# Scores of a quaternion attention over one head's 32 partitions, and the third batch's expert tiles beside the last batch's dense experts

## The reference, cut to what matters

```python
def _L1_attn_ref(x, ...):                       # quaternion attention
    q = quat_norm(quat_linear(x, qW, qb))
    k = quat_norm(quat_linear(x, kW, kb))
    v = quat_linear(x, vW, vb)
    # 16 heads of 8 features
    scores = jnp.einsum('bthd,bshd->bhts', q_, k_) * scale
    scores = scores + jnp.mean(jnp.sin(J[:T])) * 0.1
    attn = jax.nn.softmax(scores, axis=-1)
    out = jnp.einsum('bhts,bshd->bthd', attn, v_).reshape(B, T, D)
    return quat_linear(out, oW, ob)

def _L1_ffn_ref(x, gate_w, w1, b1, w2, b2):     # 8 experts, each token takes 2
    probs = jax.nn.softmax(jnp.einsum('bsd,ed->bse', x, gate_w), axis=-1)
    topk_probs, topk_idx = jax.lax.top_k(probs, 2)
    h = jax.nn.gelu(w1 of the expert @ x + b1)  # 128 -> 512
    y = w2 of the expert @ h + b2               # 512 -> 128
    return jnp.sum(y * topk_probs[..., None], axis=-2)
```

## Time and profile before

| | |
|---|---|
| median of 3 runs | 1028.57 us (1026.48 to 1032.39) |
| the profiled execution, its own time | 1028.42 us |
| its span, first to last instruction | 1026.6 us |
| granted TensorE clock, mean | 0.914 |
| PE, DVE, ACT, POOL busy | 788.0, 558.1, 486.0, 288.4 us |

### The profile page before, as it was taken

One profiled execution on the slowest core, in us unless ns is written; L12 is line 12 of the kernel. 1 busy time (PEld: TensorE's weight loads), 2 busy tenths in 40 slices (PEclk: granted clock), 3 DMA queues, 4 the chain that ended last, 5 costly groups with the idle time before them and its releaser, 6 DMA issues.

```text
span 1026.6 us, 21722 instructions
## 1 busy us (share of the span) xinstructions
PE 788.0 (77%) x8393; PEld 567.9 (55%) x8393; DVE 558.1 (54%) x1728; ACT 486.0 (47%) x1035; POOL 288.4 (28%) x366
## 2 busy tenths in 40 slices
PE   1688886778887889888989786976667576765896
PEld 0577765656665566665566552754426453365575
DVE  3255566466655374545374724776645366298145
ACT  1234352325544547754557525778343365434332
POOL 3200101000333020233020234553273675046400
PEclk9989999799998999997999988999876788889899
DMA  4400200001100001000001011010110110101100
GB/s 122 135 2 2 117 2 3 1 1 28 38 2 11 2 12 42 2 23 12 9 5 32 12 40 44 27 34 12 49 52 23 47 47 8 34 28 36 40 11 21
DMA packets 32530, 29.89 MB, mean 29 GB/s; under 512 B 9230, under 2 KB 26404, under 8 KB 32300
## 3 DMA queue, kind: packets, MB, share of 16 engines
q1 hardware_dynamic: 30636, 25.23, 8.6%
q0 software_dynamic: 1536, 3.15, 1.1%
q10 hardware_dynamic: 256, 0.13, 0.0%
HBM read 11.44 MB, written 8.52 MB: 19 GB/s over the span
## 4 chain that ended last, share of the span: by engine, by line
PE 49%; DVE 26%; issue 9%; ACT 8%; POOL 3%; ACTq 1%; another core or an unknown queue 1%; POOLq 0%; SPq 0%; DMA 0%; DVEq 0%
PE ps L1522 5%; PE ps L1667 5%; PE ps L1537 4%; PE ps L1682 4%; PE ps L1525 4%; PE ps L1450 3%; PE ps L1550 3%; PE ps L1767 3%; PE ps L1758 3%; DVE probsT L973 3%; PE ps L1617 2%; PE ps L1519 2%; ACT late L901 2%; DVE neg_max L1160 2%; DVE stats L1006 2%
## 5 line engine op out<-in xcount | busy, mean ns | idle before, releaser
L901 ACT ACTIVATE late<-ps,j_bias 128x512 f32<-128x512 f32 x256 | 173.6, 693 | 193.6 <-PE ps L1667 170.7
L1160 DVE TENSOR_REDUCE neg_max<-ps 128x2 f32<-128x32 f32 (+31 forms) x128 | 90.4, 706 | 148.2 <-PE ps L1528 144.1
L611 POOL TENSOR_SCALAR q_heads<-q_heads,head_mask 128x512 fp32r<-128x512 f32 x64 | 100.6, 1588 | 206.0 <-DMA q_heads<-q_half 205.9
L1667 PE MATMUL ps<-q_heads,k_parts 128*128 128x512 f32 x256 | 138.7, 558 | 17.1 <-ACT late L901 14.1
L828 ACT ACTIVATE probs<-ps,neg_max 128x16 f32<-128x16 f32 (+31 forms) x256 | 108.9, 483 | 26.5 <-DVE neg_max L1160 26.2
L752 ACT ACTIVATE probsT<-ps 128x128 f32<-128x128 f32 (+3 forms) x128 | 55.8, 436 | 127.3 <-PE ps L1537 113.7
L1522 PE MATMUL ps<-kT_two,q_wide 64*64 64x262 f32 (+16 forms) x1024 | 74.2, 354 | 36.3 <-DVE probsT L973 24.7
L973 DVE COPY probsT<-ps 128x128 f32<-128x128 f32 (+3 forms) x173 | 74.8, 432 | 48.2 <-PE ps L1537 24.8
L1537 PE MATMUL ps<-ident,probs 128*128 128x128 f32 x640 | 97.5, 284 | 1.0 <-ACT probs L828 1.0
L635 POOL TENSOR_TENSOR q_wide<-qT,eighth_mask 128x1024 f32<-128x1024 f32 x16 | 31.2, 1948 | 228.8 <-PE ps L1528 167.6
L1667 PEld LDWEIGHTS ps<-q_heads,k_parts 128*128 128x128 f32 x256 | 50.8, 206 | 66.6 <-ACT late L901 45.2
(11 more groups left out here) (259 smaller groups left out, 1424.4 us busy)
## 6 DMA issues: line engine op xcount, KB each, us to landing
k_parts<-k_half SPq DMA_DIRECT2D x64, 64.0 KB, 2.0
q_heads<-q_half SPq DMA_DIRECT2D x64, 64.0 KB, 2.0
x_by_expert<-q_heads SPq DMA_DIRECT2D x3, 960.0 KB, 7.6
probsT<-x_by_expert SPq DMA_DIRECT2D x45, 64.0 KB, 1.8
y_by_expert<-probsT SPq DMA_DIRECT2D x45, 64.0 KB
late<-in_L_ffn_w_dram SPq DMA_DIRECT2D x1, 2048.0 KB
w_in<-in_L_ffn_w_dram SPq DMA_DIRECT2D x1, 2048.0 KB
x_all<-in_L_attn_x_dram SPq DMA_DIRECT2D x4, 256.0 KB, 5.3
```

The costliest lines, as they stand in the source:

```text
L611: last = pool.tensor_scalar(q_heads[:, hg % 2, g, :], together.bitcast(f32), head_mask[:, g:g + 1], None, ALU.mult)
L901: nc.scalar.activation(head_probs[:, i % SLOTS, :], ps[:, banks[i % len(banks)], :], ACT.Exp, bias=j_bias[:]).then_inc(e2_ready.sem, 1)
L1160: nc.vector.tensor_reduce(neg_max[:, n % 4, :], ps[:, k:k + OCT, 0:QS * (n + 1)], axis=AXX, op=ALU.max, negate=True).then_inc(max_ready.se ...
L1667: mm(ps[:, banks[i % R], :], k_parts[:, hg, kc * P:(kc + 1) * P], q_heads[:, hg % 2, g, :], start=True, stop=True).then_inc(s2_ready.sem, 1)
```

## The change

1. `spread_group` writes the four combinations onto every fourth partition (`parts[c:P:4]`), for k and for q (`q_parts`, new, one place per group). A head's 8 features x 4 combinations then lie on 32 neighbouring partitions, and the score product takes those 32 alone. The masks on POOL, `heads_apart` and `q_heads` go. Groups 0 to 2 are spread at slot 52, group 3 at the last slot.
2. X of batch 1 runs in round 5 from slot 6 on in every third slot.
3. Behind round 5, N of batch 3 comes first; two pieces of X of batch 2 stand beside its last two pieces, and three stand behind each piece of D. This batch (`BY_GELU`) uses ACT's gelu directly: one ACT pass from PSUM in place of L933, L1336, L1338, L925, L1319.
4. D's up products rotate over two banks (0, 5), the down products over 6 and 7. The gelu table is loaded at the end of N of batch 3. C moves: batch 1 behind D pieces 0 to 2, batch 2 behind 5 to 7.

```diff
@@ plan
-                put(r, 12, "X", 1, NX, 2)
+                put(r, 6, "X", 1, NX, 3)
@@
-        for k in range(max(NX, RANKED)):
-            if k < RANKED:
-                yield ("N", LAST)
-            if k < NX:
+        for k in range(RANKED):
+            yield ("N", LAST)
+            if k >= RANKED - 2:
                 yield ("X", LAST - 1)
         for k in range(NE):
             yield ("D", LAST)
-            if k in (0, 2, 3):
+            yield from [("X", LAST - 1)] * 3
+            if k in (0, 1, 2):
                 yield ("C", LAST - 2)
-            if k in (1, 4, 5):
+            if k in (5, 6, 7):
                 yield ("C", LAST - 1)
@@ sync
+            def spread_group(b, hg):
+                if b:
+                    sp.wait_ge(s2_ready.sem, s2_ready.at(b - 1, (hg + 1) * GH * KC))
+                for c in range(4):
+                    for half, parts, which, done in ((k_half, k_parts, c // 2, k_spread), (q_half, q_parts, c % 2, q_spread)):
+                        sp.dma_start(parts[c:P:4, hg, :].bitcast(f32),
+                                     half[hg * GR:(hg + 1) * GR, which, :].bitcast(f32)).then_inc(done[hg].sem, 16)
@@ gpsimd
-            def heads(b, hg):
...
-                for g in (1, 2, 3, 0):
-                    last = pool.tensor_scalar(q_heads[:, hg % 2, g, :], together.bitcast(f32),
-                                              head_mask[:, g:g + 1], None, ALU.mult)
-                last.then_inc(heads_apart.sem, 1)
@@ scalar, by_expert
-                    if 0 <= n < NT:
+                    if 0 <= n < NT and b != BY_GELU:
...
-                                                        ps[:, 1 + (b * NT + n) % 2, m * P:(m + 1) * P], ACT.Identity,
+                                                        ps[:, 1 + (b * NT + n) % 2, m * P:(m + 1) * P],
+                                                        ACT.Gelu_apprx_tanh if b == BY_GELU else ACT.Identity,
@@ tensor, quat
-                            pe.wait_ge(heads_apart.sem, heads_apart.at(b, hg + 1))
+                            pe.wait_ge(q_spread[hg].sem, q_spread[hg].at(b + 1, 0))
...
-                        mm(ps[:, banks[i % R], :], k_parts[:, hg, kc * P:(kc + 1) * P], q_heads[:, hg % 2, g, :],
+                        rows = slice(g * GR, (g + 1) * GR)
+                        mm(ps[:, banks[i % R], :], k_parts[rows, hg, kc * P:(kc + 1) * P], q_parts[rows, hg, :],
```

More of the change, by code:

```diff
@@ L495, in spread @@
                 sp.wait_ge(k_half_ready.sem, k_half_ready.at(b, 1))
+                sp.wait_ge(q_half_ready.sem, q_half_ready.at(b, 1))
                 for hg in range(HG - 1):
-                    spread_k(b, hg)
-                sp.wait_ge(q_half_ready.sem, q_half_ready.at(b, 1))
-                spread_q(b, 0)
+                    spread_group(b, hg)
                 yield
[L501 to L511, removed]
+                spread_group(b, HG - 1)
                 yield
@@ L553, in all_experts @@
                 yield
-            take({"S": spread, "Q": quat, "X": by_expert, "C": sums, "D": all_experts})
+            take({"S": spread, "X": by_expert, "C": sums, "D": all_experts})
             sp.wait_ge(x_stored.sem, x_stored.at(B, 0))
@@ L717, in sums @@
                 yield
-            take({"R": relative, "A": attention, "W": weights, "S": spread, "Q": quat, "N": norm, "X": by_expert,
-                  "C": sums})
+            take({"R": relative, "A": attention, "W": weights, "N": norm, "X": by_expert, "C": sums})
         def copy_pT(eng, copy, o, done, b, n):
@@ L950, in all_experts @@
                             act.wait_ge(moe_y_ps.sem, e - 1)
-                        nc.scalar.activation(moe_h[:, e % 2, m, :], ps[:, n % NUP, :], ACT.Gelu_apprx_tanh,
+                        nc.scalar.activation(moe_h[:, e % 2, m, :], ps[:, UP_BANKS[n % NUP], :], ACT.Gelu_apprx_tanh,
                                              bias=b1T[:, m, e:e + 1]).then_inc(moe_h_ready.sem, 1)
+                    if e == 0:
+                        act.wait_ge(gatesT_ps.sem, 1)
+                        copy(gates_T, ps[0:NE, DOWN_BANKS[1], :].rearrange("p (t s) -> p t s", t=T)
+                             ).then_inc(gatesT_ready.sem, 1)
                     yield
@@ L1329, in by_expert @@
                             dve.wait_ge(y_stored[(b * NT + n) % 2], 16 * ((b * NT + n) // 2))
-                        nc.vector.scalar_tensor_tensor(out=yx[:, (b * NT + n) % 2, :], in0=wc[:, (b * NT + n) % 4, W3:W3 + P], scalar=2.0,
+                        nc.vector.scalar_tensor_tensor(out=yx[:, (b * NT + n) % 2, :], in0=wc[:, (b * NT + n) % 4, W3:W3 + P],
+                                                       scalar=1.0 if b == BY_GELU else 2.0,
                                                        in1=ps[:, AM, 0:P], op0=ALU.mult, op1=ALU.add
@@ L1742, in by_expert @@
                     if 0 <= n < NT:
-                        pe.wait_ge(hx_ready.sem, hx_ready.at(b, n + 1))
+                        if b == BY_GELU:
+                            pe.wait_ge(hb_ready.sem, hb_ready.at(b, n + 1))
+                        else:
+                            pe.wait_ge(hx_ready.sem, hx_ready.at(b, n + 1))
                         if b * NT + n:
@@ L1772, in all_experts @@
                 pe.wait_ge(e2_ready.sem, e2_ready.at(B, 0))
-                pe.wait_ge(hb_ready.sem, hb_ready.at(LAST, 0))
+                pe.wait_ge(attn2_ready.sem, attn2_ready.at(B, 0))
                 up(0)
+                pe.wait_ge(b7_free, fill_no["N", LAST, 9] + 1)
                 pe.wait_ge(gates_ready.sem, 1)
                 for t in range(T):
-                    last = nc.tensor.transpose(ps[0:NE, 3, t * P:(t + 1) * P], gates[:, t, :], ident[:])
+                    last = nc.tensor.transpose(ps[0:NE, DOWN_BANKS[1], t * P:(t + 1) * P], gates[:, t, :], ident[:])
                 last.then_inc(gatesT_ps.sem, 1)
@@ L1780, in all_experts @@
                 for t in range(T):
-                    last = mm(ps[:, 3, t * P:(t + 1) * P], gates_T[:, t, :], b2_sb[:], start=True, stop=True)
+                    last = mm(ps[:, DOWN_BANKS[1], t * P:(t + 1) * P], gates_T[:, t, :], b2_sb[:], start=True, stop=True)
                 last.then_inc(accb_ps.sem, 1)
                 for e in range(NE):
+                    yield
                     if e + 1 < NE:
```

67 lines of the change are left out of this document (18 added, 49 removed).

## The result

The kernel after takes 1057.78 us (median of 4 runs, 1054.02 to 1059.97), the kernel before 1030.05 beside it: a ratio of 1.0269 with a 95% interval from 1.0223 to 1.0314. It is 28 us slower, where 13 us faster was forecast, and lies outside the range. A second set of runs gave 1.0299 (1.0237 to 1.0361).

The account below looks back on a forecast made before the run. PE was taken to bound rounds 2 and 3, waits round 5. From 1028.4 us, +17 (score shape) - 2 (masks) - 20 (round 5) - 8 (tail) = -13 gave 1015 us, range 990 to 1036.

Parts of the forecast that it names:

- the sum's first term: Scores on PE: shape changes cost 0 to 34 us; half, +17, taken because the chain is on PE 49% of the span.
- The shape's price for one score: On PE, a 32-row score between two 128x128 products costs about 0.29 us more; next product 0.40 or more behind.
- rival (b): Rounds 2 to 4: shape changes lie fully on the path, the kernel gets slower, about 1045 us; chance 0.15.
- a cold clock in round 5 on 10 of them: Slower rival's addition to 34 us of shape changes: round 5's low clock (0.79) repeats; together taken as 40 us.
- The growth by over 10 us and the clock under 0.88: Signs of a wrong forecast: rounds 2 to 4 each grow over 10 us, or their granted clock falls below 0.88.
- parts 2 and 3: Round 5 (wider tile spacing, mask wait gone), 20 us less, and the new order behind it, 8 us less.
- Nothing is saved on PE: Scores on PE: the same 256 products of 512 columns remain, so no PE time is gained.
- The masks: POOL's mask work beside DVE's small steps lengthens some of them; its going saves 2 us (0 to 5).
- Off the chain nearly everywhere: POOL's mask work, 16 groups of 6.2 us, 99 us in all, hardly stands in the chain.
- Round 5: Fewer waits for tile weights, earlier weight copies and wider tile spacing: 20 us less (8 to 28).
- The tail: Behind round 5: the last norm begins at 1010 against 1018.9, 8 us less.
- 2.2 more: Behind round 5: batch 1's gathers, standing before tile 5, add 2.2 us to the groups of X pieces.

Follow-up runs that it names:

- row means: Ratios to the kernel before, averaged over four plans (old, wider spacing, new tail, both): masked 128-row scores 0.995, zeroed tiles 0.985, 32-row scores 1.026.
- zeroed tiles: Kernel before, masks replaced by DMAs putting each head's queries on its own 32 partitions of otherwise zero tiles, full 128-row products: 0.9818; with new plans 0.9827 to 0.9885.
- old plan: Round 5 spacing and tail left as in the kernel before; with only the scores changed, 32 rows gave 1.0297, DMA-filled zero tiles 0.9818.
- The 64 rows: Kernel after with score products over 64 rows, each summing two heads' scores (output not the reference's): 1045.85 us, ratio 1.0236.
- the pair of added products: Kernel after with one more product ahead of each score in rounds 4 and 5: on 128 rows 1059.79 us (1.0367), on 32 rows 1075.37 us (1.0458).
- without the plans: Kernel before with the 32-row scores alone, its round 5 and tail as they were: 1056.58 us, ratio 1.0297.
- the spacing: Kernel before, masks kept, with only the new wider spacing of the tiles in round 5: 1022.79 us, ratio 0.9941.
- the plans alone: Kernel before with the wider tile spacing in round 5 and the new tail, masked 128-row scores kept: 1019.91 us, ratio 0.9915.
- the new tail alone: Kernel before, masks kept, with only the new order of work behind round 5: 1024.95 us, ratio 0.9941.

## Why the prediction was wrong

**The step that failed** is the sum's first term, "I take half, 17 us", and that the clock was left out of it. On the path the 32-row score costs about 4.1 of 100 (row means 1.026 to 0.985), 42 us; the single pairs of ratios give 28 to 49. Cut by rounds, scores on 32 rows against zeroed tiles, old plan: 6.4, 8.9, 24.2, 9.1, then 3.7 behind the last score.

- The shape's price for one score was right: 0.28 us between 128*128 neighbours, forecast 0.29, with the next product 0.43 behind the score and the score 0.20 behind the last product (forecast 0.40 or more, and 0.20). PE's busy time grows by 10.8 and 13.4 us in rounds 2 and 3, more than the forecast's 34 us over four rounds would give. But "half, because PE holds half the chain" used an average over the span. Rounds 2 and 3 are bound by PE, and 15.3 of these 24 us lay on the path; in round 3 the clock had a share in it (0.93 against 0.97).
- The clock was a repeat in rival (b), at 0.15 with shape changes, as "a cold clock in round 5 on 10 of them". It fell in round 4 already (0.88 to 0.74). The growth by over 10 us and the clock under 0.88, which the prediction named as signs of being wrong, both show in that round, and in no other of the three. Two thirds of the loss are in rounds 4 and 5, where the old clock already went up and down. The 64 rows, and the pair of added products, show that the fall goes with the rows of the score. The earlier trace rows showed that the clock was already low there (0.79 in round 5); the step from "a quarter of the array's rows" to "less of what keeps the clock" was missing.
- (b) named the right side and the first cause; its place, rounds 2 to 4, holds three quarters of the loss. Its sum is added up wrongly: 1028 + 40 - 2 - 14 is 1052, not 1045. That its 40 is near the 42 is in part luck, as it took 34 for the shape and 6 for the clock in round 5, while the larger part of the loss is where the clock fell. The gains of parts 2 and 3, taken there at half, come to nothing measurable on 32-row scores (1.0297 without the plans, 1.0269 and 1.0299 with them).
- "Nothing is saved on PE" was not quite so: the 26 pairs of scores in rounds 4 and 5 that ran at once saved PE 0.3 us or more each, since two 128-row scores start 0.31 to 0.34 us apart at the upper clock; that makes 8 us of PE as an estimate. It was lost beside the rest.

**The masks** were priced at 2 us, beside what of them was in round 5. Their going is worth about 1 in 100 of the time (row means 0.995 to 0.985), 10 us; single pairs give 6 to 19. Between before and the zeroed tiles 10.8 of these were in round 5, 5.5 in round 4. "Off the chain nearly everywhere" was read from where POOL stands in the chain; what a mask did to the steps behind it does not stand there. Which steps these were is not shown: the xn wait of 8.2, now 4.6, is 4.8 with the masks in and the tiles spaced wider.

**Round 5**, forecast -20 with its mask's going: -5 (1022.79 against 1027.67) from the spacing, and nothing once the masks are gone. The named wait for POOL did go, but PE then waits 12.4 for the same products by another name. The two gains don't add (1004.99 us without the masks, 1015.81 with the wider spacing too); that both edits take away the same slack is the likely reason, not a shown one. In the kernel after this wait is 4.7, under the 9 forecast, and the round is still longer (142.2 against 136.4).

**The tail**, forecast -8: from the first transposes of N to the end of the span the plans alone take 130.5 us in place of 137.6, which is -7.1, and the new tail alone gave -3 (1024.95 against 1027.67). The kernel after takes 133.0 and shows the steps. Its chain:

```profile
943.60 1.73 PE ps L1695 x8
945.33 4.93 PE ps L1718 x8
...
958.21 11.11 another core or an unknown queue
...
976.62 3.62 PE ps L1718 x8
980.25 3.57 PE ps L1729 x32
983.93 0.89 PE ps L1695 x8
...
990.46 3.62 PE ps L1718 x8
```

N's first transposes are at 923.76, so the first tile is 20 behind them (forecast 19.5); a piece of D takes 7.19 (7.2), a group of three tiles 6.5 (6.4). The step that was off is batch 1's gathers ahead of a tile's weights, "2.2 more": DVE stands still for 11.1, ACT for 7.9 and PE for 4.0. On POOL:

```profile
958.76 0.97 POOL L666 DMA_INDIRECT q_rel<-y_by_expert,row_no  x1
...
968.49 0.61 POOL L650 COPY probsT<-w1T 128x512 f32 x1
```

Eight gathers, 9.7 us, stand between the weights of two tiles, and it is only behind them that DVE goes on; the profile doesn't name what it waits for. The last norm starts 125.3 behind N (forecast 121, before 129.9); DVE ends its weighted sums 5.8 us after PE's last product (forecast 6).

**What stays open.** Kernels whose work is the same up to a point came out 4 to 10 us apart in single rounds of their profiles. Mostly the longer round had the lower clock, but not in round 4 of the zeroed tiles (149.4 us at 0.85, 145.1 at 0.84); what decides it was not found. How the 33 us of rounds 4 and 5 split between shape and clock was not measured either. So the sizes of the spacing's and the tail's gains (0 to 6 us), and which plan is best on zeroed tiles, are not settled. Settled is the sign of the rest: 32-row scores cost 28 us or more against zeroed tiles with the same plan, and all four kernels with zeroed tiles are faster than both the kernel before and the one after (ratios 0.982 to 0.989).

## What to carry to other kernels

Before a matmul is cut to fewer rows, look at what it saves and at what it takes away. Alone it saved nothing here (0.50 us on 32 rows, 0.48 on 128); it saves only where the next one on another strip stands right behind it, which a plan must arrange. What it takes away is the continuity of shape with its neighbours, paid on both sides, and the part of PE's work that holds the granted clock, paid by every product around it. Look for the second cost in the stretches where the clock already moves, not in the full ones. If data must be kept apart by head, let the DMA that moves it anyway write into zeroed tiles, and keep the full-row product. And an engine that is off the chain is not free: price it by the waits behind it, and don't add two gains that may close the same wait.

## What the runs showed of the hardware

- A score between 128*128 products costs 0.28 us more on 32 rows than on 128 (0.43 and 0.58 against 0.32 and 0.41 to its neighbours). On 64 rows rounds 2 and 3 are as long as on 32, so this is the change of shape and not the size. The Trainium skill (TensorEngine Tiling, Key Properties) says that a change of tiling mode drains the array; these rows agree.
- The granted clock follows the rows that products fill: rounds 4 and 5 at 0.87 and 0.83 with 128-row scores, 0.81 and 0.80 with 64, 0.74 and 0.67 with 32. With PE 79% busy, 70 us on end were granted 1.2 GHz (744.0 to 814.7 in the kernel after).
- Two 32-row scores on different strips, one right behind the other, start 3 or 4 ns apart (26 times in the kernel after); two 128-row scores at the upper clock start 0.31 to 0.34 us apart.
- 128 more full-row products of 512 columns made rounds 4 and 5 together 3.2 us longer in the profiles (312.8 against 309.6) and the whole kernel 7 to 10 us by the ratios: the higher clock paid for most of them.
